# First attention: the projections of each pair issued one unit earlier in the order of work

## What is computed

```python
q = _rope((x @ wq).reshape(B, S, 32, 128), pos)
k = _rope((x @ wk).reshape(B, S, 8, 128), pos)
v = (x @ wv).reshape(B, S, 8, 128)
scores = einsum('bqhgd,bshd->bhgqs', qg, k) * sm_scale      # qg: 8 groups of 4 heads
allowed = (j <= i) & (j > i - 128)
attn = softmax(where(allowed, scores, neg))
out = einsum('bhgqs,bshd->bqhgd', attn, v).reshape(B, S, 4096) @ wo
x = layernorm(x + out)
```

## Time and profile before

| | us |
|---|---|
| median of 3 runs | 2449.51 |
| span of the profiled execution, first to last instruction | 2436.7 |
| TensorE (PE) busy | 1735.8 (71%) |
| VectorE (DVE) busy | 1618.9 (66%) |
| ScalarE (ACT) busy | 1291.9 (53%) |
| POOL busy | 1019.0 (42%) |
| first attention, first scores to the start of the last pair | 55.88 to 822.33 |

### The profile page before, as it was taken

How to read it: one execution, slowest core, us unless ns; L and a number is a source line. 1 busy time by engine, 2 the same in 40 slices (tenths; PEclk the granted TensorE clock), 3 DMA queues, 4 the chain that set the end, 5 groups by cost and what they waited for, 6 DMA issues and landing times. The chain is left out here.

```text
span 2436.7 us, 25968 instructions
## 1 busy us (share of the span) xinstructions
PE 1735.8 (71%) x7274; PEld 1296.7 (53%) x7274; DVE 1618.9 (66%) x3711; ACT 1291.9 (53%) x3343; POOL 1019.0 (42%) x699
## 2 busy tenths in 40 slices
PE   5888888888888869997685455425644633566997
PEld 4777777777777658886552222212322311334885
DVE  3677766776666645556435888898788879742335
ACT  3556555465554433333337777876677788433221
POOL 3435445354443435553203343346433334632442
PEclk9999999999999979998855667657766756788998
DMA  3112111111110112221400000010000000001111
GB/s 148 31 42 69 53 56 47 41 55 65 56 46 17 57 61 95 103 77 53 113 20 7 7 7 1 12 16 7 7 7 7 7 1 7 1 1 44 39 52 47
DMA packets 33570, 96.40 MB, mean 40 GB/s; under 512 B 4048, under 2 KB 16720, under 8 KB 29264
## 3 DMA queue, kind: packets, MB, share of 16 engines
q1 hardware_dynamic: 33456, 95.20, 11.8%
HBM read 87.84 MB, written 7.34 MB: 39 GB/s over the span
## 5 line engine op out<-in xcount | busy, mean ns | idle before, releaser
L198 PE MATMUL PS<-AR 128*128 128x512 f32 (+2 forms) x2568 | 559.5, 373 | 172.6 <-issue 71.6
L198 PE MATMUL PS<-XT,AR 128*128 128x512 f32 x2472 | 633.6, 412 | 24.1 <-POOL AR L796 12.3
L198 PEld LDWEIGHTS PS<-AR 128*128 128x128 f32 x2568 | 454.0, 199 | 270.3 <-issue 158.2
L198 PEld LDWEIGHTS PS<-XT,AR 128*128 128x128 f32 x2472 | 482.1, 198 | 140.0 <-issue 14.4
L1235 POOL TENSOR_TENSOR AF<-AF 128x512 f32<-128x512 f32 (+3 forms) x64 | 148.4, 2319 | 487.5 <-DVE AF L1440 487.5
L1043 PE MATMUL PS<-AR,XT 48*128 48x128 f32 (+3 forms) x256 | 129.0, 504 | 139.6 <-DVE BF L1303 72.5
L1176 ACT ACTIVATE AF<-PS 128x512 f32<-128x512 f32 x160 | 94.0, 594 | 252.4 <-PE PS L1056 130.5
L546 POOL TENSOR_TENSOR AF<-AF 128x512 f32<-128x512 f32 x80 | 103.2, 1291 | 255.8 <-ACT AF L338 255.8
L1071 PE MATMUL PS<-AF,BF 128*128 128x512 f32 x320 | 189.7, 697 | 20.8 <-ACT AF L1176 20.8
L1091 PE MATMUL PS<-BF,AF 128*128 128x1 f32 x24 | 7.0, 362 | 265.2 <-DVE BF L1401 265.2
L552 POOL TENSOR_TENSOR AF<-AF 128x512 f32<-128x512 f32 (+1 forms) x64 | 107.5, 1680 | 178.2 <-DVE AF L681 178.2
(11 more groups left out here) (171 smaller groups left out, 3635.0 us busy)
## 6 DMA issues: line engine op xcount, KB each, us to landing
AF<-in_mean_w SPq DMA_DIRECT2D x48, 448.0 KB, 3.3
AF<-in_ffn_w SPq DMA_DIRECT2D x14, 1536.0 KB, 6.3
AF<-in_attn_w SPq DMA_DIRECT2D x9, 1536.0 KB, 6.7
AF<-in_attn_w SPq DMA_DIRECT2D x9, 1024.0 KB, 5.2
AF<-in_ffn_w SPq DMA_DIRECT2D x11, 769.0 KB, 4.4
XT<-rope_scratch SPq DMA_DIRECT2D x96, 64.0 KB, 2.8
rope_scratch<-BF SPq DMA_DIRECT2D x20, 256.0 KB, 2.3
AF<-in_x SPq DMA_DIRECT2D x8, 256.0 KB, 4.1
```

The costliest lines, as they stand in the source:

```text
L198: last = nc.tensor.matmul(dst, lhs(a, c), rhs(m, c), start=(first and k == 0), stop=(k == 3 * n - 1 and not more))
```

## The change

The projections of a pair are issued one unit earlier on all engines. In unit (b, i) the item that is issued is now that of tile j = (i + 1) % 4: in units 0 to 2 still for the next pair (q1 and v, q2 and the turning, q3), in unit 3 for the pair after next (q0 and k), whose batch is the unit's own. `upcoming` gives pair, batch, group of the weights, tile, and whether it exists. The prologue gets q0 and k of the second pair on every engine, and `PIECES` splits the next group's weights one unit earlier (q0 and k two units earlier, the output weights where they were).

```diff
@@ -314,8 +314,15 @@
             pool.wait_ge(A[f"w{kind}_hi"], (4 * g + h if kind == "q" else g) + 1)
             nc.gpsimd.tensor_tensor(dst[:, 1], src, f32(dst[:, 0]), ALU.subtract).then_inc(A[f"w{kind}_lo"], 1)
 
-        PIECES = {1: [("o", 0, 0)], 2: [("q", 0, 1), ("k", 0, 1)], 3: [("q", 1, 1), ("v", 0, 1)],
-                  4: [("q", 2, 1)], 5: [("q", 3, 1)]}
+        PIECES = {0: [("q", 0, 1), ("k", 0, 1)], 1: [("o", 0, 0)], 2: [("q", 1, 1), ("v", 0, 1)],
+                  3: [("q", 2, 1)], 4: [("q", 3, 1)]}
+
+        def upcoming(g, u, last_group):
+
+            b, j = u // QT, (u + 1) % QT
+            step = 1 if j > 0 else 2
+            exists = not last_group or (b == 0 and j > 0)
+            return 2 * g + b + step, (b + step) % 2, g + (b + step) // 2, j, exists
 
         def groups(eng, body):
 
@@ -396,22 +403,20 @@
                     last.then_inc(A0["scores"], 1)
                     if not (first and u == 0):
                         turn_p(n - 1, (u - 1) % QT)
-                    nb, j = (b + 1) % 2, i
-                    ng = g if b == 0 else g + 1
-                    has_next = not (last_group and b == 1)
+                    tb, nb, ng, j, has_next = upcoming(g, u, last_group)
                     if has_next:
-                        pe_proj_item(pe, ng, bb + 1, nb, "q", j, 5 * (bb + 1) + head_item(j))
+                        pe_proj_item(pe, ng, tb, nb, "q", j, 5 * tb + head_item(j))
                     if not (first and u < 2):
                         oproj(n - 2, g if u > 1 else g - 1)
                     if not (first and u == 0):
                         pv(n - 1, (u - 1) % QT, ((u - 1) // QT) % 2)
                     if has_next:
                         if j == 0:
-                            pe_proj_item(pe, ng, bb + 1, nb, "k", 0, 5 * (bb + 1) + 1)
+                            pe_proj_item(pe, ng, tb, nb, "k", 0, 5 * tb + 1)
                         if j == 1:
-                            pe_v(pe, ng, bb + 1, nb, 0)
+                            pe_v(pe, ng, tb, nb, 0)
                         if j == 2:
-                            pe_vturn(pe, bb + 1)
+                            pe_vturn(pe, tb)
 
             def turn_p(n, i):
                 pe.wait_ge(A0["pnorm"], n + 1)
@@ -444,7 +449,8 @@
                     pe_v(pe, 0, 0, 0, 0)
                 if j == 2:
                     pe_vturn(pe, 0)
-            pe.wait_ge(A0["v_lo"], 1)
+            pe_proj_item(pe, 0, 1, 1, "q", 0, 5)
+            pe_proj_item(pe, 0, 1, 1, "k", 0, 6)
             groups(pe, body)
             n = NU * KVH0
             turn_p(n - 1, QT - 1)
@@ -497,17 +503,18 @@
                     vcopy(0)
                 if j == 2:
                     v_hi(0, 0)
+            for r, k, h in items0(1, 0):
+                rope_act1(act, r, src0(k), slot_of(k, 1, 0))
+                rope_hi(r, k, 1, 0)
 
             def body(g, first, last_group):
                 for u in range(NU):
                     b, i = u // QT, u % QT
                     n = NU * g + u
-                    bb = 2 * g + b
-                    nb, j = (b + 1) % 2, i
-                    has_next = not (last_group and b == 1)
+                    tb, nb, ng, j, has_next = upcoming(g, u, last_group)
                     if not (first and u == 0):
                         pt_hi(n - 1, (u - 1) % QT)
-                    its = items0(bb + 1, j) if has_next else []
+                    its = items0(tb, j) if has_next else []
                     if its:
                         rope_act1(act, its[0][0], src0("q"), slot_of("q", nb, j))
                     if 1 <= u < 7:
@@ -527,9 +534,9 @@
                         rope_act1(act, its[1][0], src0("k"), slot_of("k", nb, j))
                         rope_hi(its[1][0], "k", nb, j)
                     if has_next and j == 1:
-                        vcopy(bb + 1)
+                        vcopy(tb)
                     if has_next and j == 2:
-                        v_hi(bb + 1, nb)
+                        v_hi(tb, nb)
                     for kind, h, ahead in PIECES.get(u, []):
                         if (ahead and last_group) or (first and not ahead):
                             continue
@@ -573,15 +580,15 @@
             for j in range(G0):
                 for r, k, h in items0(0, j):
                     rope_sin(r, slot_of(k, 0, j))
+            for r, k, h in items0(1, 0):
+                rope_sin(r, slot_of(k, 1, 0))
 
             def body(g, first, last_group):
                 for u in range(NU):
                     b, i = u // QT, u % QT
                     n = NU * g + u
-                    bb = 2 * g + b
-                    nb, j = (b + 1) % 2, i
-                    has_next = not (last_group and b == 1)
-                    its = items0(bb + 1, j) if has_next else []
+                    tb, nb, ng, j, has_next = upcoming(g, u, last_group)
+                    its = items0(tb, j) if has_next else []
                     if its:
                         rope_sin(its[0][0], slot_of("q", nb, j))
                     pnorm(n, i)
@@ -643,15 +650,17 @@
                     rope_lo(r, k, 0, j)
                 if j == 2:
                     v_lo(0, 0)
+            for r, k, h in items0(1, 0):
+                rope_cos(r, k)
+                rope_rot(r, slot_of(k, 1, 0))
+                rope_lo(r, k, 1, 0)
 
             def body(g, first, last_group):
                 for u in range(NU):
                     b, i = u // QT, u % QT
                     n = NU * g + u
-                    bb = 2 * g + b
-                    nb, j = (b + 1) % 2, i
-                    has_next = not (last_group and b == 1)
-                    its = items0(bb + 1, j) if has_next else []
+                    tb, nb, ng, j, has_next = upcoming(g, u, last_group)
+                    its = items0(tb, j) if has_next else []
                     if not (first and u < 3):
                         yadd(n - 3, (u - 3) % NU)
                     if last_group and u >= 3:
@@ -688,7 +697,7 @@
                         rope_rot(its[1][0], slot_of("k", nb, j))
                         rope_lo(its[1][0], "k", nb, j)
                     if has_next and j == 2:
-                        v_lo(bb + 1, nb)
+                        v_lo(tb, nb)
 
             groups(dve, body)
             n = NU * KVH0
```

## The result

The kernel after takes 2381.35 us, median of 4 runs (2377.4 to 2382.12), against 2448.1 before (2445.84 to 2454.55): ratio 0.9727, 95% interval 0.9705 to 0.9749; the medians are 66.8 us apart. 2379 was forecast. The span of the profiled execution is 2375.6 us (2436.7 before).

A forecast was written before the change was run, and what follows sets the result against it. TensorE's 3.5 us wait for the rope's residual at each pair's start, with the slow clock behind it, was taken as the bound. Gains of 65.5 us in 14 periods, 70 with the ends, gave 2379 us, range 2345 to 2412.

The forecast's parts named there:

- The wait at the pair's start: TensorE's 3.5 us gap before a pair's first scores, for VectorE's residual (line 616), 52.8 us together, goes.
- The schedule of a pair: Four units: 42.0 us of work and 3.9 of waits, period 45.9 to 46.0; with output weights 47.1 to 47.2.
- steps 2 to 6: Around a pair: masks of units 0 and 1 at 14.4 and 23.25; TensorE waits of 0.5, 1.8 and 1.5 us.
- mask(3): VectorE's mask addition of unit 3, zero of the pair's schedule; in the first pair about 92 instead of 95.04.
- The clock behind waits of 1.5 to 2.2 us: TensorE's new waits of 1.5 to 2.2 us cost no clock, as a 1.97 us wait left it at 2.4 GHz.
- rival 2: TensorE's clock still falls once a pair, behind a wait of 1.5 to 2.2 us: 34 us, 2413; chance 13%.
- The first pair: Prologue gets two projections and two ropes; first mask about 65; 3 us lost to 6 gained, 3 gained taken.
- The span, and what lies around it: Profiled span 2436.7 becomes 2367 us; median 12.8 above it, for what lies outside first and last instruction.
- Rival 1: The new TensorE waits don't come: pairs of 43.8 and 45.7 us, 2355; region 2330 to 2355 has 16%.
- Rival 3: Softmax chain longer than laid out, 2 us a pair, 2407; sign: wait over 2.5 us at line 420; 7%.
- Rivals 4 and 5: TensorE at 1.2 GHz for much of the stage, 2484 us, 3%; wait for unit 0's mask takes whole gap, 2449, 3%.
- The terms of a pair's work: TensorE's scores, transposes, projections, output projections with P times V and turning over four units, summed to 42.0 us.

The follow-up runs named there:

- the filled gap: Kernel before, with 14 extra 128x512 matmuls issued ahead of the wait for the rope at each pair's start: 2415.89 us, ratio 0.9874.
- v later, pieces first: Kernel after, with v and its turning one unit later and ScalarE taking the weight pieces ahead of the copies of v: 2347.24 us, ratio 0.9578.
- the two steps behind it: Added to v one unit later: weight pieces ahead of the copies of v, 2347.24 us; then also output addition ahead of the rope of k, 2338.14 us.

## Why the prediction was right, point by point

**The wait at the pair's start: right.** Line 616 (623) has no place among TensorE's waits any more.

**The schedule of a pair: right.** The rows of after put steps 2 to 6 within 0.2 us; in the pair with the output weights the wait is 1.9 instead of 2.2 and the period 46.9 instead of 47.2. From mask(3) of the first pair (96.05) to that of the fifteenth (749.94) are 653.9 us; 653 was forecast, 718.3 were before.

```profile
96.05 1.21 DVE L672 TENSOR_TENSOR AF<-PS,AF 128x1024 f32<-128x1024 f32 x1
...
749.94 1.19 DVE L672 TENSOR_TENSOR AF<-PS,AF 128x1024 f32<-128x1024 f32 x1
```

**The clock behind waits of 1.5 to 2.2 us: partly wrong.** I took from one row that a wait of 2 us leaves the clock at 2.4 GHz; all seven such waits of before do (18 matmuls in 4.37 to 4.40 us), but not those of after. In the seven pairs with output weights a wait of 1.76 and one of 1.89 us stand 4 us apart (1.68 and 1.88 in the last group). In four the matmuls behind kept the full clock, in three they didn't (starts 181.26, 461.16 and 741.12). The same place in two groups, then its windows (us, TensorE busy, clock):

```profile
275.34 5.85 PE L198 MATMUL PS<-AR 128*128 128x512 f32 x30 [1.89 <-POOL AR L315]
...
461.16 7.40 PE L198 MATMUL PS<-AR 128*128 128x512 f32 x30 [1.87 <-POOL AR L315]
```

```profile
275.40:281.20 5.80, 5.78 (x30) 1.00 0.83 284
```

```profile
461.20:468.60 7.40, 7.40 (x32) 0.77 0.71 266
462.80:464.40 1.60, 1.60 (x5) 0.50 0.91 333
```

The last window, inside the 7.40 us, is at 1.2 GHz: the prediction's sign of being wrong, a clock of 0.5 behind a wait under 2.3 us, did show.

Such a pair takes 48.05 instead of 46.93 us (two of the three; the last group's has no pair behind it to measure to). This is rival 2 in a small measure, and the direction in which the Trainium skill, TensorE: Matmul & The Clock Gate (A second HAM failure mode), pointed. The shorter wait of 1.4 us showed no fall in seven pairs. Why the same code loses the clock in one group and keeps it in the next stays open. That the sum came out nevertheless is luck, an offset: 47.2 was forecast for a pair without a fall and 46.93 measured, 1.9 us in seven pairs, against 2.2 us lost in two falls.

**The first pair: wrong, 4 us.** The bounds were 3 lost to 6 gained, and I took 3 gained, mask(3) at 92; it came at 96.05, 1 us later than before. mask(0) came at 65.25, as laid out, but TensorE, with only 3 matmuls of output work yet to do in unit 1, stood 4.40 us for the normalisation in unit 2, and behind that the clock fell:

```profile
80.83 1.97 PE L425 MATMUL PS<-AF 128*128 128x128 f32 x8 [4.40 <-POOL AF L559]
```

```profile
80.80:90.00 9.20, 9.17 (x32) 0.68 0.00 0
```

The 8 transposes took 1.97 us instead of 1.09 and the query projection behind them 5.00 instead of 3.04: 2.8 of the 4 us. I had followed VectorE there, not TensorE's idle time. This is the largest mis-sized term.

**The span, and what lies around it: wrong reading, right median.** Forecast was a span of 2367; it is 2375.6. The next stage's first transpose starts at 809.97 instead of 876.67, so the first attention gained 66.7 us where 70 was forecast: 64.4 in the 14 periods (65.3 forecast), 3.3 behind them (1.5 forecast), 1.0 lost ahead of them (3 gained forecast). The span gained 5.6 less than that, in the stages behind, which the change doesn't touch: from that transpose to the end before took 1560.0 us, after 1565.6, and in the experiments 1565.7 (the filled gap) to 1575.6 (v later, pieces first), though no kernel edits them. By what they differ I did not test. Nor did the 12.8 us between span and median lie outside first and last instruction: for the profiled run of the kernel after the difference is 1.8 us (2377.4 against 2375.6), and it is 1.8 in the recorded runs of before too. The profiled execution of before, 2436.7 us, was a quick one. The forecast of the median doesn't suffer from that, since it is the median before less 70.

**Where the gain comes from.** The same 3502 matmuls, from 35 us to the start of the next stage, kernel before and then after (us, TensorE busy, clock):

```profile
35.00:876.60 841.60, 718.66 (x3502) 0.94 0.14 49
```

```profile
35.00:809.90 774.90, 686.93 (x3502) 0.98 0.15 53
```

TensorE is busy 31.7 us less with the same matmuls, nearly all of it the clock, and idle 35.0 us less (122.9 to 88.0); together the 66.7. The waits agree: from 101.5 us (52.8 + 17.6 + 17.1, and 14.0 for line 315) to 66.5 (47.0 + 13.2 + 6.3). The filled gap, up to the same point, gains 30.4 us (876.67 to 846.26), all of it clock, and net of its own six falls behind the 2.0 us waits.

**The rivals.** Rival 1 (no new waits) fell: 47.0 us stand at line 425. Rival 3 fell with the schedule; its sign, a wait over 2.5 us for the normalisation, shows only in the first pair (2.60 and 4.40 us) and in the last group (up to 3.85 us, where the kernel before had one of 3.8 too). Rivals 4 and 5: no trace of them.

**Slips in the working.** The terms of a pair's work add up to 41.9 us, not 42.0, and 718.3 less 653 is 65.3, not 65.5. In rival 4 the clock of 0.68 belongs to the projection at 363.30, not to the one of 4.09 us, whose window shows 0.72; and a clock 3 to 6% below full means that TensorE was at 1.2 GHz for twice that share of the time. None of them moves the forecast.

## What to carry to other kernels

When a wait at the start of a stage's period is removed by issuing its producer earlier, lay out the whole period from durations of the trace, engine by engine, and look for the units that become short: part of the wait comes back there. Work placed to even out the units is worth a good part of the move again: here v one unit later about 25 us, and 43 with the two steps behind it, beside the 67 of the move. Everything that the moved item reads must move with it: with the splits left behind, 59 of the 67 us were lost. And price a wait of TensorE with the clock behind it: each gap of 3.5 us cost 1.7 or 3.2 us more through slow matmuls.

## What the runs showed of the hardware

- A wait of 1.9 us, 4 us behind another of 1.8, let the clock fall in three of seven repetitions of the same code and left it in four; with the old splits it fell in one of seven; 1.4 us in that place, in none of seven.
- A single wait of 2.0 us before the same 18 matmuls left the clock in all seven groups of the kernel before (4.37 to 4.40 us), and lost it in two of seven with v one unit later (5.99 and 6.00 us) and in six of seven with the earlier gap filled (5.97 to 6.02 us). So the length of one wait doesn't decide it; what does is open.
- Behind waits of 3.7 to 3.9 us (q1 with late splits, seven times) and of 4.4 us (the first pair) the matmuls ran slow each time. The slow level need not start with the first matmul: at 309.73 of the kernel before the 12 score matmuls behind the 3.50 us gap took 1.55 us, and only the transposes and the projection behind them ran slow (4.09 us instead of 3.05).
- VectorE's subtraction of line 623, both inputs in SBUF, takes 2.17 us while POOL normalises 128x1024 and 0.69 us in the rope of k, when POOL is idle; the chain of a full unit holds the long one. It ends 0.55 us behind the end of POOL's instruction, whether that takes 1.89 us (316.99 against 316.44) or 1.04 (350.07 against 349.53), as if it waited that instruction out.
